# Attention and mixture of experts on one core: another order inside the turns of a group loop, and five multiplies moved from VectorE to GpSimd

## The reference, cut to what matters

```python
# x: (4, 1024, 256); ctx: (4, 77, 256); 8 experts, hidden 512, top 2
x = x + tanh(g_xattn) * (softmax(mask(layernorm(x) @ ctx.T / 16)) @ ctx @ W.T + b)
xf = layernorm(x).reshape(4096, 256)
routing = softmax(xf @ router_w.T)                    # 8 experts
top_w, top_i = top_k(routing, 2);  top_w /= sum(top_w)
y_e = (silu(xf @ w_gate[e].T) * (xf @ w_up[e].T)) @ w_down[e].T
x = x + tanh(g_ffn) * sum over the two chosen e of top_w * y_e
```

## Time and profile before

| what | value |
|---|---|
| median of 3 runs | 424.16 us (423.8 to 424.55) |
| the profiled execution's own time | 426.31 us |
| its span, first to last instruction | 424.6 us |
| mean granted TensorE clock | 0.991 of full speed |
| busy: PE / DVE / ACT / POOL | 97% / 74% / 66% / 66% |

### The profile page before, as it was taken

The page is one execution under the profiler, slowest core; times in us unless marked ns, Lnnn a source line. Parts: engine busy times, 40 slices in busy tenths (PEclk is TensorE's granted clock), DMA queues, the critical chain, the costliest instruction groups (busy, mean ns, idle before and its releaser), DMA issues.

```text
span 424.6 us, 9945 instructions
## 1 busy us (share of the span) xinstructions
PE 410.6 (97%) x3249; PEld 378.0 (89%) x3249; DVE 314.2 (74%) x694; ACT 281.7 (66%) x569; POOL 278.8 (66%) x269
## 2 busy tenths in 40 slices
PE   7999899998999999999999999999999999999993
PEld 2887775544999999999999999999999999999993
DVE  6557999986687777677777777777777776777772
ACT  2468877513576767777767766777767677767673
POOL 7004754754367677777777776677777777677775
PEclk9899999999999999999999999999999999999998
DMA  6846967751786777733334333434333434333433
GB/s 185 298 154 203 298 204 245 260 197 48 244 215 146 167 170 170 177 64 50 59 54 62 64 62 50 61 52 63 69 57 50 63 51 66 68 53 50 63 55 64
DMA packets 34624, 50.25 MB, mean 118 GB/s; under 512 B 3846, under 2 KB 26023, under 8 KB 34599
## 3 DMA queue, kind: packets, MB, share of 16 engines
q0 software_dynamic: 13440, 19.19, 27.1%
q1 hardware_dynamic: 19815, 29.84, 22.2%
q10 hardware_dynamic: 1344, 0.92, 0.7%
HBM read 32.24 MB, written 17.70 MB: 118 GB/s over the span
## 4 chain that ended last, share of the span: by engine, by line
PE 47%; POOL 23%; issue 15%; DVE 7%; ACT 3%; POOLq 2%; DMA 2%; ACTq 0%; DVEq 0%
POOL out_rows L516 15%; PE GT L1247 11%; PE UP L1247 11%; PE Y L1275 10%; POOL xt L504 7%; PE S L1121 4%; PE W L1096 3%; PE O L1170 2%; PE XT L1237 2%; ACT ex L607 2%; DMA out_rows<-y,idx 1%; PE ET L1096 1%; DVE at_low L842 1%; POOLq L533 1%; POOLq L60 1%
## 5 line engine op out<-in xcount | busy, mean ns | idle before, releaser
L516 POOL DMA_INDIRECT out_rows<-y,idx x68 | 159.6, 2347 | 65.6 <-ACT y L678 52.1
L1039 DVE TENSOR_TENSOR gu<-raw,gu 128x1024 fp32r<-128x1024 f32 x70 | 85.8, 1226 | 62.3 <-ACT gu L654 58.9
L1247 PE MATMUL GT<-xtT,gu 128*128 128x256 f32 x828 | 113.6, 286 | 0.4 <-DVE gu L1039 0.4
L1247 PE MATMUL UP<-xtT,gu 128*128 128x256 f32 x828 | 110.6, 283 | 0.0
L1247 PEld LDWEIGHTS GT<-xtT,gu 128*128 128x128 f32 x828 | 103.8, 191 | 0.8 <-DVE gu L1039 0.7
L1247 PEld LDWEIGHTS UP<-xtT,gu 128*128 128x128 f32 x828 | 104.3, 192 | 0.0
L1275 PE MATMUL Y<-dn,hT 128*128 128x256 f32 x816 | 103.6, 283 | 0.0
L1275 PEld LDWEIGHTS Y<-dn,hT 128*128 128x128 f32 x816 | 100.4, 192 | 0.1
L504 POOL DMA_INDIRECT xt<-xn_rows,idx x74 | 74.3, 1004 | 29.3 <-issue 22.2
L654 ACT CAST gu<-raw 128x1024 fp32r x68 | 70.9, 1042 | 30.7 <-PE UP L1247 28.5
L1060 DVE TENSOR_TENSOR hid<-hid,UP 128x512 f32<-128x512 f32 x68 | 46.5, 684 | 9.7 <-PE UP L1247 9.7
(11 more groups left out here) (168 smaller groups left out, 395.7 us busy)
## 6 DMA issues: line engine op xcount, KB each, us to landing
raw<-in_weights SPq DMA_DIRECT2D x32, 384.0 KB
xn_rows<-pay SPq DMA_DIRECT2D x8, 528.0 KB, 3.3
xTg<-in_xT SPq DMA_DIRECT2D x8, 512.0 KB, 3.9
xg<-in_x SPq DMA_DIRECT2D x8, 512.0 KB, 5.9
out_rows<-xg SPq DMA_DIRECT2D x8, 512.0 KB, 4.0
xt<-xn_rows,idx POOLq DMA_INDIRECT x74
out_rows<-y,idx POOLq DMA_INDIRECT x68
kr<-in_ctx_rows SPq DMA_DIRECT2D x1, 308.0 KB
```

The source lines that it names most:

```text
L516: gp.indirect_dma_start(out=out, out_offset=bass.IndirectOffsetOnAxis(ap=idx[:, 2 * j + t:2 * j + t + 1], axis=0), in_=y[:, j % 2, t, :], ...
L1039: return tt(out=out, in0=whole, in1=high.bitcast(F32), op=ALU.subtract)
L1247: last = mm(bank[:, h * PT:(h + 1) * PT], gu[:, pw, q, c, w, h * P:(h + 1) * P], xtT[:, b, px, c], start=(h == 0 and c == 0 and n == 0), s ...
```

## The change

It has these parts.

- Inside a turn on DVE: `share(k-1)` now stands between `lg1` and `negmean2`, and `negmean2` ahead of the last three `add_rows`; `negated_means(k+3)` and `low_places(k-1)` stand behind `ve` in place of ahead of it; `values(k+1)` stands behind `nb`, where `values` stood before `ve` in turn 0 and at the end of turns 0 and 1.
- On PE: `ranks(k)` comes ahead of `scores(k+4)`, `values(k+2)` behind it in place of right behind `attention`, and there are fewer `keep_busy` matmuls (none in place of 10 in turn 0, 3 for 5, 2 for 4, 13 for 18).
- `coded` of groups 0 to 4 runs on POOL, behind `weighed(k)` of `k` = 1 to 5. `coded` of groups 5 and 6 stays on DVE. Group 7's `at_low` is made on ACT, by 8 Square and 8 Relu activations of 128x128.
- The list: what was left of group 6's `at_low` and `coded` goes ahead of the wait for the counts, the last group's ranks go ahead of the experts' starts, and the numbers are coded so that `idx` takes one instruction less.

```diff
+            def coded(k):
+                pool.wait_ge(rows_hot, (k + 1) * CU)
+                of = at_low[:, k * CU // 2:(k + 1) * CU // 2]
+                gp.tensor_tensor(of, of, by_two(code[:].rearrange("p g c t -> p (g c t)"), k, 0, CU), ALU.mult).then_inc(low_by_pool, 1)
+
             for k in range(GROUPS):
                 routed(k)
                 normed_rows(k)
                 weighed(k)
+
+                if 1 <= k <= BY_POOL:
+                    coded(k - 1)
...
+            for u in range(CU):
+                nc.scalar.activation(apart[:, u], iota_p[:, :, 0], ACT.Square, bias=low_last[:, u:u + 1], scale=-1.0
+                                     ).then_inc(apart_ready, 1)
+            for u in range(CU):
+                act.wait_ge(apart_ready, u + 1)
+                last = nc.scalar.activation(at_low[:, (UNITS - CU + u) // 2, :, u % 2], apart[:, u], ACT.Relu,
+                                            bias=code_last[:, 0, u % G:u % G + 1], scale=code_last[:, 1, u % G:u % G + 1])
...
                 summed = mark(tt(out=lg1[:], in0=lg0[:], in1=sr[:, q], op=ALU.add))
+                if k > 0:
+                    share(k - 1)
+                after(summed)
+
+                ts(negmean2[:, q], lg1[:, :, NE], -1.0 / D, None, ALU.mult).then_inc(negmean2_ready, 1)
                 add_rows(1).then_inc(rows_added, 1)
-                after(summed)
-                ts(negmean2[:, q], lg1[:, :, NE], -1.0 / D, None, ALU.mult).then_inc(negmean2_ready, 1)
...
-                    values(1)
-                    after(squared)
-                else:
-                    share(k - 1)
-                if n + 1 < GROUPS:
-                    negated_means(n + 1)
...
-                    low_places(k - 1, masked)
                 dve.wait_ge(ssq2_ready, k + 1)
...
-                coded(behind)
+                if n + 1 < GROUPS:
+                    negated_means(n + 1)
+                if k > 0:
+                    low_places(k - 1, masked)
+                if behind >= BY_POOL:
+                    coded(behind)
                 refine(n)
...
+                if k + 1 < BATCH:
+                    values(k + 1)
...
             for c in range(UNITS // CHUNK):
-                if c == UNITS // CHUNK - 1:
-                    at_lows(last_group, 0, CU)
-                    coded(last_group)
```

More of the change, by code:

```diff
@@ L37 @@
 CU = TOPK * G
+BY_POOL = 5
 CHUNK = 2 * CU
@@ L155, in moe_flamingo @@
         col = sb("col", [P, UNITS], F16, a)
-        sign = sb("sign", [P, TILES], F32, a)
+        lift = sb("lift", [P, TILES], F32, a)
         size = sb("size", [P, TILES], F32, a)
         none = sb("none", [P, TILES], F32, a)
-        shift = sb("shift", [P, TILES], F32, a)
         J = sb("J", [1, PAIRS], F32, a)
@@ L247, in moe_flamingo @@
         low_ready = sem("low_ready")
+        low_by_pool = sem("low_by_pool")
+        rows_hot = sem("rows_hot")
+        apart_ready = sem("apart_ready")
+        last_low_ready = sem("last_low_ready")
         counts_ready = sem("counts_ready")
@@ L286, in slot_of, with by_two @@
             return g % XS * G
+        def by_two(of, k, lo, hi):
+            return of.rearrange("p (u two) -> p u two", two=2)[:, k * CU // 2 + lo // 2:k * CU // 2 + hi // 2].unsqueeze(2
+                   ).to_broadcast([P, (hi - lo) // 2, P, 2])
         def rows(g, t):
@@ L440, in _ @@
                              fill=0.0, base=0, channel_multiplier=-1)
-            gp.iota(code[:, 0:GROUPS // 2], [[G * P, GROUPS // 2], [0, TOPK], [P, G]], base=1, channel_multiplier=1, **exact)
-            gp.iota(code[:, GROUPS // 2:], [[-G * P, GROUPS // 2], [0, TOPK], [-P, G]], base=-1, channel_multiplier=-1, **exact)
-            gp.iota(pad_row[:], [[1, 1]], base=N + 1, channel_multiplier=1, **exact)
+            gp.iota(code[:, 0:GROUPS // 2], [[G * P, GROUPS // 2], [0, TOPK], [P, G]], base=-(N // 2), channel_multiplier=1, **exact)
+            gp.iota(code[:, GROUPS // 2:], [[G * P, GROUPS // 2], [0, TOPK], [P, G]], base=1, channel_multiplier=1, **exact)
+            gp.iota(code_last[:, 0], [[P, G]], base=N // 2 - G * P + 1, channel_multiplier=1, **exact)
+            gp.iota(code_last[:, 1], [[-P, G]], base=-(N // 2 - G * P + 1), channel_multiplier=-1, **exact)
+            gp.iota(pad_row[:], [[1, 1]], base=N - (N // 2 - 1), channel_multiplier=1, **exact)
             gp.iota(iota_e[:], [[1, NE]], base=0, channel_multiplier=0, **exact)
@@ L678, in weigh @@
                     nc.scalar.mul(y[:, s % 2, t], Y[:, t, 0:D], xt[:, 2 * s + t, bass.ds(e + CW, 1)]).then_inc(y_ready, 1)
+            act.wait_ge(places_ready, GROUPS)
+            act.wait_ge(pool_consts, 4)
+            for u in range(CU):
[5 more added lines that the diff above has]
+                                            bias=code_last[:, 0, u % G:u % G + 1], scale=code_last[:, 1, u % G:u % G + 1])
+            last.then_inc(last_low_ready, 1)
             nc.scalar.preload_act_table_set("silu_and_others")
@@ L841, in at_lows @@
                 at = k * CU // 2
-                rows_hot[0] = mark(tt(out=at_low[:, at + lo // 2:at + hi // 2],
-                                      in0=iota_p[:].unsqueeze(1).to_broadcast([P, (hi - lo) // 2, P, 2]),
-                                      in1=by_two(low[:], k, lo, hi), op=ALU.is_equal))
+                tt(out=at_low[:, at + lo // 2:at + hi // 2], in0=iota_p[:].unsqueeze(1).to_broadcast([P, (hi - lo) // 2, P, 2]),
+                   in1=by_two(low[:], k, lo, hi), op=ALU.is_equal).then_inc(rows_hot, hi - lo)
             def coded(k):
@@ L849, in coded @@
                     return
-                after(rows_hot[0])
+                dve.wait_ge(rows_hot, (k + 1) * CU)
                 of = at_low[:, k * CU // 2:(k + 1) * CU // 2]
@@ L965, in _ @@
                     inverted = reciprocal_sums(n)
-                if k < 2:
-                    values(k + 2)
             last_group = GROUPS - 1
             at_lows(last_group - 1, 0, 4)
+            at_lows(last_group - 1, 4, 8)
+            coded(last_group - 1)
             share(last_group)
@@ L1013, in _ @@
             listed = L[:, LIST:LIST + TILES]
-            upper = mark(ts(sign[:], listed, 0.0, -2.0, ALU.is_lt, ALU.mult))
+            lower = mark(ts(lift[:], listed, 0.0, float(N // 2 - 1), ALU.is_lt, ALU.add))
             empty = mark(ts(none[:], listed, 0.0, pad_row[:], ALU.is_equal, ALU.mult))
-            after(upper)
-            sized = mark(stt(out=size[:], in0=sign[:], scalar=1.0, in1=listed, op0=ALU.add, op1=ALU.mult))
+            after(lower)
+            lifted = mark(stt(out=size[:], in0=listed, scalar=1.0, in1=lift[:], op0=ALU.mult, op1=ALU.add))
             after(empty)
[L1019 to L1022, removed]
+            after(lifted)
+            tt(out=idx[:], in0=size[:], in1=none[:], op=ALU.add).then_inc(idx_ready, 1)
             empty = mark(ts(second_empty[:], L[0:1, LIST:LIST + TILES].rearrange("p (j t) -> p j t", t=2)[:, :, 1], 0.0, 16.0,
@@ L1123, in scores @@
                 last.then_inc(scores_ready, 1)
-            keep_busy(4, W)
+            keep_busy(7, W)
             transpose_keys(0, M)
-            keep_busy(3, W)
+            keep_busy(1, W)
             pe.wait_ge(pool_consts, 3)
@@ L1196, in _ @@
                 attention(k + 1)
-                if k < 2:
-                    values(k + 2)
-                keep_busy(10 if k == 0 else 5, ET)
+                if k > 0:
+                    keep_busy(3, ET)
                 if k + 2 < GROUPS:
                     transpose_exp(k + 2)
+                ranks(k)
                 if k + 4 < GROUPS:
@@ L1207, in _ @@
                     keep_busy(9, W)
-                ranks(k)
-                if k >= 2:
-                    keep_busy(4, W)
+                if k + 2 < BATCH:
+                    values(k + 2)
+                if k >= BATCH - 1:
+                    keep_busy(2, W)
             keep_busy(22, W)
@@ L1219, in _ @@
             ranks(GROUPS - 1)
-            keep_busy(18, W)
+            keep_busy(13, W)
             for u in range(UNITS):
@@ L1225, in _ @@
                 if u % CU == 0:
-                    pe.wait_ge(low_ready, u // CU + 1)
+                    if u == UNITS - CU:
+                        pe.wait_ge(last_low_ready, 1)
+                    elif u // CU < BY_POOL:
+                        pe.wait_ge(low_by_pool, u // CU + 1)
+                    else:
+                        pe.wait_ge(low_ready, u // CU + 1 - BY_POOL)
                 last = mm(L[:, LIST:LIST + TILES], at_low[:, u // 2, :, u % 2], at_tile[:, u // 2, :, u % 2], start=(u == 0), stop=(u == UNITS - 1))
```

29 lines of the change are left out of this document (14 added, 15 removed).

## The result

| kernel | median | runs |
|---|---|---|
| before | 424.41 us | 423.49 to 426.23, 22 runs |
| changed | 426.25 us | 423.32 to 430.08, 22 runs |

The ratio is 1.0039, with a 95% interval of 1.0023 to 1.0055: slower by 0.4%. Ratios and their intervals leave out executions over 1.5% above the fastest of the same kernel, medians and ranges keep them. The prediction had 426.7. The profiled execution of the changed kernel took 427.69 us, its span is 425.9.

A forecast was written before the change was run, and what follows sets the result against it. Third stage PE-bound, so the first fetch's shift decides; POOL's multiply holds DVE's refine in five turns. -3.4 + 8.2 - 0.3 - 2.0 = +2.5 us on a 424.16 median gives 426.7; range 422.5 to 431.

The forecast's parts named there:

- Third stage unchanged, all in the shift of the first fetch: Third stage: PE busy 149.80 of 150.30 us, length kept; the change's effect equals the shift of the rows fetch at 99.68.
- First batches, -3.4: Turns 0 and 1: ve without values ahead gives -2.0, no DVE wait for scores -1.4; together -3.4 us.
- the absolute 39.0: First batches: the time in us at which POOL's picks of turn 1 was forecast to stand.
- The -1.4 of turn 1: Turn 1 on DVE: 1.46 us idle for scores goes, as the negated means now stand behind ve; -1.4 us.
- What is held: Turns 2 to 6: DVE's two-SBUF-input refine waits for POOL's whole multiply, taken as 2.1 us (1.7 to 2.8).
- The rival of a hidden multiply: Turns on POOL: small DVE products not held, multiply fits POOL's idle time; total -6.7, 417.5 us; chance 0.12.
- Turns of 9.4 us, +8.2: Five turns: refine to picks 2.37, picks to end of pay 4.92, multiply 2.1; 9.4 against 7.75 us, +8.2.
- The small moves, 0.2 a turn: Inside a turn on DVE: negated means, cast of low and share moved, so ve comes 0.2 us earlier.
- Turn 7, -0.3: Turn 7: no POOL multiply lies in it; the small moves give -0.3 us.
- The list, -2.0: The list: -1.8 us from moved at_low and coded work, bounds -1.2 and -2.6, and -0.2 from idx; together -2.0.
- The clock: Rival: PE gaps of some 3 us could lower its clock, or rows load late; 1 to 4 us more; chance 0.08.
- the prediction's three places: Trace rows for krow, at_low and rt0v, cited as DVE instructions kept from finishing by a running POOL instruction.

The follow-up runs named there:

- the repeated run before: The kernel before, unchanged, profiled once more: 424.22 us, span 422.5.
- the first profile: The original profile of the kernel before, unchanged: 426.31 us, span 424.6, with the scores of group 0 at 3.58 us and a clock of 0.67 from 9 to 14 us.
- at a steady clock: The changed kernel with nine in place of three keep_busy matmuls ahead of the transposes in turns 1 to 6: 424.36 us, ratio 1.0008.
- the memset: On the changed kernel with all multiplies on DVE and nine fillers, a write-only POOL memset of a spare tensor where the multiply stood: 419.71 us, ratio 0.9889.

## Why the prediction was right, and where two errors cancelled

The forecast was the likeliest case and came out 0.45 us above the measured median. By its own steps:

- **Third stage unchanged, all in the shift of the first fetch**: right, 324.9 us behind it in both profiles. The fetch came at 101.01, forecast 102.2; against the repeated run before it moved by +2.96.
- **First batches, -3.4**: right in size. `picks` of turn 1 stand at 37.15 for 40.77, -3.6. `ve` of turn 0 came from 28.99 to 26.87, -2.1 for the -2.0 forecast. Of the 1.8 us that the absolute 39.0 was off, 1.6 are the first profile's late scores. The -1.4 of turn 1 was put down to DVE's order alone; PE's order, which brings the scores 3.0 us sooner, has a part in it, and the two were not tried apart.
- **What is held**: right in three of the five turns of the changed profile, where one instruction of `refine` lasts until POOL's multiply ends, to 0.04 us. In turns 3 and 4 it is one ahead of it, with one input. The rival of a hidden multiply, which would have given 417.5, is refuted: 418.24 is what the kernel takes with the multiply gone, 433.71 with two.
- **Turns of 9.4 us, +8.2**: this term was mis-sized. With the clock steady a turn takes 8.85. Of `picks` to the end of `pay` 4.92 became 4.78, the multiply 1.89 for 2.1, and from the end of the hold to `picks` 2.19 for 2.37 (turn 2 of the changed profile): 4.78 + 1.88 + 2.19 = 8.85. The forecast had counted the 2.37 from the start of `refine`, but when the hold ends, the held instruction is done as well: from the end of `rt0v` to `picks` are 66.08 - 63.88 = 2.20 in the earlier trace rows too. Five such turns cost 44.26 - 38.75 = +5.5, not +8.2.
- **The small moves, 0.2 a turn**: too small. With the multiplies on DVE and the clock steady (the run with the start's fillers as before) the five turns take 74.13 - 37.15 = 36.98, 7.40 each for 7.75, so -0.35 a turn. The multiply's own price is 8.85 - 7.40 = 1.45 a turn, 7.3 us.
- **Turn 7, -0.3**: nothing (6.66 for 6.70).
- **The list, -2.0**: right at a steady clock, 9.99 for 11.83, -1.84, of which ACT's part 1.2. The hold by POOL's `pay` is about 0.6 us here, not up to 1: `low_i`, `cum` and `starts` take 0.41, 0.38 and 0.59 us, in the changed profile, where the counts are late, 0.17, 0.21 and 0.42. In the profiled run of the changed kernel only 11.83 - 11.30 = 0.5 was left, with the counts late.
- **The clock**: this was put into a rival of its own at 0.08, as 1 to 4 us on top of the forecast, and it happened. Turn 4 took 1.6 us more than at a steady clock, the list 1.3. The gap that opened on PE was 1.35 us, not some 3. In the median it is 426.25 - 424.36 = 1.9 us.

Against the kernel before the steady sum is -4.05 (36.72 - 40.77) + 5.5 - 0.05 - 1.84 = -0.4, a change that does nothing; measured is 424.36 for 423.96, ratio 1.0008. The +2.5 of the forecast was thus 2.7 too much in the turns, and nothing for the clock, which brought about 2 back. That the two cancelled is luck. The step that failed is the one that left the clock out of the sum: a gap on PE follows from the held `refine` by the same chain as the late `picks`, and the mean clock was lower in all 22 executions.

Of the Trainium skill (SBUF — State Buffer, Who interferes with whom) the trace agrees with two statements: that a DVE instruction with two SBUF inputs is blocked in full by one of GpSimd that reads (1.76 for 0.17 us), and that it is not by one that only writes (0.16 and 0.18 us under the memset). The same section of the Trainium skill says that a `tensor_scalar` or a cast can enter a mode that takes both ports, and then contends with GpSimd; the holds of `rstd` (0.62 us under the memset), `ve` (1.55) and the cast of `low` (1.39) under the multiply fit that, though no trace shows the mode. Of the prediction's three places only two bear on the rule of two inputs: `krow` has one input and the iota beside it reads nothing, so it belongs with `rstd`. And only `rt0v`'s end matches POOL's to 0.03 us, the other two come 0.21 and 0.13 behind it. From the Trainium skill (GPSIMD Engine Reference, Elementwise — side-by-side cycle accounting), whose figure is for a float32 add, the prediction's estimate was 2.25 us for the multiply; the rows have 1.89 for this float16 product, and the measurement decides.

## What to carry to other kernels

An engine's idle time is not free room: ask what another engine will be doing in it, and where two engines hold each other, put the long instruction beside the other's PSUM reads, or cut it into pieces, and not ahead of a short chain that others wait for. Here 1.89 us that fit into 2.98 of idle time cost 1.45 us a turn. Where a hold opens a gap on PE, price the clock too, or fill the gap. The multiplies left on DVE turn a change of +0.4% into one of -1.4% (418.24 us), with five fillers -1.6% (417.38 us); what the fillers add there is within the noise.

## What the hardware showed that I had not expected

- Eight-element instructions are held as fully as long ones, as forecast: 0.17 us become 1.84. Not forecast was that one-input ones are too: `ve` takes 1.55 and the cast of `low` 1.39, both 0.16 unheld.
- A one-input TENSOR_SCALAR of 128x4 float32 is held even by an instruction of POOL that reads nothing (0.62 us, up to the memset's end), while its two-input neighbours are not.
- A gap on PE doesn't always cost the clock. With DVE's multiplies and three fillers a gap of 1.08 us left the 16 scores behind it at 2.02 us, the next of 1.28 us was followed by scores of 3.01, and the turn behind that took 10.49 us. The same kernel ran from 417.5 to 420.5 us. In the run with the start's fillers as before (417.25 us) a gap of 1.35 us, as long as that of the changed kernel, left the clock at 1.00.
